# Layer-2 field products in four row strips with a turn of their own on the y banks, and W2 loaded in turned pieces

## The chip, the cores and the metric

One core of a Trainium2 chip runs the whole kernel. The metric is the device time of one execution in microseconds. Engines are named as in the profile: PE is the matrix engine (PEld its weight loads), DVE the vector engine, ACT the scalar engine, POOL the general engine, SP the engine that only issues DMAs.

## What is computed

The input x has 512 rows of 64 fields with 16 elements each. Three layers of a compressed interaction network follow one another; each multiplies the previous layer's channels with all 64 fields, element by element, and mixes the products with a weight matrix of 128 outputs. The output is the sum over the 16 elements of each layer.

```python
for W, b in params:                      # W0: 128 x 64*64, W1 and W2: 128 x 128*64
    z = jnp.einsum('bhd,bfd->bhfd', x_vec, input)
    z = z.reshape(B, h * f, d)
    x_vec = jnp.einsum('oc,bcd->bod', W, z) + b[None, :, None]
    outs.append(x_vec.sum(axis=2))
return jnp.concatenate(outs, axis=1)     # 512 x 384
```

## The kernel before

**Tiling.** A tile is 8 batch rows x 16 elements = 128 columns. Four tiles make a group of 512 columns, and there are 16 groups, each a body that is written out for all engines. In a body the step e runs over 4 tiles x 16 chunks (e = 16 j + c); a chunk is four fields.

**Layer 0** of the next group is spread over the current group: the symmetric products of the fields are made in 17 pieces z (t = 0 to 16). SP copies shifted rows of x into z (L372), POOL multiplies them (L453), ACT and DVE split every second piece into two rounded parts (L526, L718), and PE adds each piece to the PSUM bank l0 at the steps of AHEAD_AT (AHEAD_FIRST_AT in the first group), whole pieces as one f32 matmul (L934), split ones as three rounded ones (L913, tile l).

**Layer 1** is the bulk. For each chunk PE makes y = W1 times x1, three 512-column matmuls (L913, tile y), into one of four PSUM banks. Then the chunk is weighted with its four fields and summed over chunks: chunks in HELPED by ACT into prod (L673) and by POOL into pacc (L461, L463), chunks in SCALED in place by ACT (L662) and added by DVE in one operation (L754), all others by DVE alone, four operations a chunk (L769, L767). PE may write a bank again only when the chunk that was there four chunks ago has been read (chunk, L1042 and L1044). At a tile's end POOL adds acc and pacc and folds them to x2 (combine, L469 to L474).

**Layer 2** needs only sums over elements. For the tile before, at c = 12 (LAYER2_AT), PE multiplies x2 with bd, a copy of the fields masked by batch row, in two halves of 64 partitions, 260 columns each (layer2, L1033), into the two banks of l2p. ACT copies the result into gram and sums (layer2_out, L563 and L565) and makes the next bd in own_rows (L652). Every four groups gram holds 128 batch rows, and PE multiplies it with w2t in 64 f32 matmuls, eight parts of eight (quarter, L1021), which use the bank xt. The turned fields use the same bank (turn_fields, L991, at TURN_AT, directly behind a layer2).

**Weights.** W0, W1 and W2 arrive in rows by output. W0 is folded by DVE (add_pairs, L851) and turned by PE in the front; W1 is turned by PE in 16 chunks in the first tile of the first group (turn_w1, L968), W2 in 16 chunks in the steps 14 to 29 of the first group (turn_w2, L1010, copied out by ACT, L582). SP loads W1 (L387), ACT loads W0 (L512) and, in the first group, W2 (L595).

**The end.** After the last chunk DVE adds pacc (L896) and reduces to x2 (L899); then follow the last layer2, its copy, the last quarter, its copy to sums (L571), three transposes (L1001), their copy (L577) and the store (L419).

## Time and profile before

| what | value |
|---|---|
| time, median of 3 runs | 1092.88 us (1091.29 to 1093.42) |
| the profiled execution's own time | 1091.6 us |
| its span, first to last instruction | 1089.5 us |
| busy share of PE, PEld, DVE, ACT, POOL | 98%, 74%, 81%, 65%, 79% |
| PE share of the chain that ended last | 90% |
| mean granted clock of PE | 0.997 |

The span is the profiled execution from its first to its last instruction; 2.1 us lie around it. Busy time is the union of an engine's instructions. Matmuls are pipelined and the end of one is modelled, so the distance between two starts tells more than one duration. A record of an f32 matmul stands for half of it: one matmul leaves two records.

### The profile page before, as it was taken

Reading aid. Unit: us, or ns where it says so; the run is one execution under the profiler, and the core shown is the slowest. Engines: PE = TensorE matmul, PEld = TensorE weight load, DVE = VectorE, ACT = ScalarE, POOL = GpSimd, SP = SyncE. Lnnn points to the kernel's source line nnn. Section 1 sums busy time; section 2 is a strip of 40 time slices with the busy share of each in tenths; the row PEclk is TensorE's granted clock in tenths of the full one; section 3 lists DMA queues with packets and bytes.
Section 4 is the critical chain, followed back from the end, with each engine's and each line's share of the span. In section 5 each row is a group of like instructions: output and inputs, shape, how many; then the busy total and the mean of one; then the engine's idle time right before and its main releaser. Section 6 shows DMA issues by size and latency. Waiting matters only on the chain.

```text
span 1089.5 us, 18056 instructions
## 1 busy us (share of the span) xinstructions
PE 1064.6 (98%) x4783; PEld 803.5 (74%) x4783; DVE 877.3 (81%) x2673; ACT 710.3 (65%) x2447; POOL 859.6 (79%) x727
## 2 busy tenths in 40 slices
PE   5999999999999999999999999999999999999997
PEld 5777777777778777777778777777778877777676
DVE  5768989889874888989894798989886598888881
ACT  4666767676764767767673676777675576767770
POOL 2668997989884897989985799898987589898550
PEclk9999999999999999999999999999999999999998
DMA  7942423332322323323241232433332133320000
GB/s 275 245 92 81 101 71 71 96 76 78 66 70 58 76 78 69 85 57 97 66 87 40 56 97 66 88 84 69 94 79 59 47 69 97 76 79 28 1 23 8
DMA packets 108327, 85.88 MB, mean 79 GB/s; under 512 B 71040, under 2 KB 73824, under 8 KB 108096
## 3 DMA queue, kind: packets, MB, share of 16 engines
q1 hardware_dynamic: 106832, 78.17, 29.3%
q10 hardware_dynamic: 1392, 6.55, 1.9%
q8 instruction: 38, 0.62, 0.2%
q14 instruction: 65, 0.53, 0.2%
HBM read 14.75 MB, written 0.79 MB: 14 GB/s over the span
## 4 chain that ended last, share of the span: by engine, by line
PE 90%; DVE 3%; ACT 2%; DMA 2%; POOL 1%; issue 1%; ACTq 0%; SPq 0%; DVEq 0%; POOLq 0%
PE y L913 62%; PE l L934 9%; PE l L913 8%; PE xt L1021 5%; PE l2p L1033 4%; DVE acc L769 2%; DMA gram<-in_L_rec_W_dram 1%; PE l2p L1010 1%; ACT y L662 1%; DMA z<-xg 1%; ACT prod L673 1%; POOL z L453 1%; DVE gram L851 1%; PE l L922 0%; POOL pacc L463 0%
## 5 line engine op out<-in xcount | busy, mean ns | idle before, releaser
L769 DVE SCALAR_TENSOR_TENSOR acc<-y,x0t,acc 128x128 f32<-128x128 f32 x2048 | 559.8, 341 | 101.8 <-PE y L913 99.1
L673 ACT ACTIVATE prod<-y,x0t 128x128 f32<-128x128 f32 x1280 | 365.8, 379 | 157.4 <-PE y L913 148.6
L913 PE MATMUL y<-w1h,x1h 128*128 128x512 f32 x1024 | 464.6, 454 | 2.2 <-DVE acc L769 1.4
L913 PE MATMUL y<-w1h,x1l 128*128 128x512 f32 x1024 | 402.1, 393 | 0.0
L913 PE MATMUL y<-w1l,x1h 128*128 128x512 f32 x1024 | 400.6, 391 | 0.0
L453 POOL TENSOR_TENSOR z<-z,xg 128x512 f32<-128x512 f32 (+2 forms) x272 | 352.5, 1300 | 32.8 <-DMA z<-xg 32.8
L463 POOL TENSOR_TENSOR pacc<-pacc,prod 128x512 f32<-128x512 f32 x192 | 268.0, 1396 | 79.7 <-ACT prod L673 78.3
L913 PEld LDWEIGHTS y<-w1h,x1h 128*128 128x128 f32 x1024 | 193.2, 189 | 96.8 <-issue 26.5
L662 ACT ACTIVATE y<-y,x0t 128x128 f32<-128x128 f32 x512 | 142.6, 342 | 157.4 <-PE y L913 157.2
L913 PEld LDWEIGHTS y<-w1l,x1h 128*128 128x128 f32 x1024 | 192.8, 188 | 59.3 <-issue 28.8
L913 PEld LDWEIGHTS y<-w1h,x1l 128*128 128x128 f32 x1024 | 192.1, 188 | 43.0
L754 DVE TENSOR_TENSOR acc<-y,acc 128x512 f32<-128x512 f32 x128 | 88.3, 690 | 64.6 <-ACT y L662 61.4
L718 DVE TENSOR_TENSOR zl<-z,zh 128x512 fp32r<-128x512 f32 (+1 forms) x128 | 126.9, 991 | 7.1 <-ACT zh L526 4.5
L934 PE MATMUL l<-z,w0t 128*128 128x512 f32 (+1 forms) x256 | 128.8, 584 | 0.0
L469 POOL TENSOR_TENSOR pacc<-pacc,acc 128x512 f32<-128x512 f32 x63 | 87.4, 1387 | 42.4 <-DVE acc L754 34.5
L461 POOL TENSOR_TENSOR pacc<-prod 128x512 f32<-128x512 f32 x64 | 90.0, 1406 | 37.7 <-ACT prod L673 37.5
L526 ACT CAST zh<-z 128x512 fp32r<-128x512 f32 (+1 forms) x128 | 81.4, 636 | 10.9 <-POOL z L453 7.7
L652 ACT ACTIVATE bd<-x0t,own_half 128x64 f32<-128x64 f32 x256 | 69.1, 359 | 0.0
L1021 PEld LDWEIGHTS xt<-gram,w2t 128*128 128x128 f32 x512 | 62.3, 195 | 3.6 <-ACT sums L565 1.5
L1021 PE MATMUL xt<-gram,w2t 128*128 128x128 f32 x512 | 62.7, 279 | 0.8 <-ACT sums L565 0.8
L767 DVE TENSOR_SCALAR acc<-y,x0t 128x128 f32<-128x128 f32 x192 | 54.9, 341 | 0.0
L934 PEld LDWEIGHTS l<-z,w0t 128*128 128x128 f32 x256 | 47.8, 188 | 9.6
(85 smaller groups left out, 673.0 us busy)
## 6 DMA issues: line engine op xcount, KB each, us to landing
z<-xg SPq DMA_DIRECT2D x480, 128.0 KB, 2.4
w2t<-in_L_rec_W_dram SPq DMA_DIRECT2D x8, 512.0 KB, 7.1
gram<-in_L_rec_W_dram ACTq DMA_DIRECT2D x8, 512.0 KB, 7.4
xg<-in_r_input_dram SPq DMA_DIRECT2D x30, 128.0 KB, 3.8
z<-xg SPq DMA_DIRECT2D x32, 96.0 KB, 5.9
z<-xg SPq DMA_DIRECT2D x15, 192.0 KB
gram<-in_L_rec_W_dram ACTq DMA_DIRECT2D x1, 2048.0 KB, 9.2
out_dram<-z SPq DMA_DIRECT2D x4, 192.0 KB, 1.9
```

Of the source, the lines that this page charges most:

```text
L453: nc.gpsimd.tensor_tensor(to[0:rows, :], to[0:rows, :], xg[0:rows, cols], ALU.mult).then_inc(z_made, 1)
L461: nc.gpsimd.tensor_tensor(pacc[:], prod[:, 0], prod[:, 1], ALU.add).then_inc(pool_step, 1)
L463: nc.gpsimd.tensor_tensor(pacc[:], pacc[:], prod[:, h % HSLOTS], ALU.add).then_inc(pool_step, 1)
L469: nc.gpsimd.tensor_tensor(pacc[:], pacc[:], acc[:, slot], ALU.add).then_inc(pool_step, 1)
L662: last = nc.scalar.activation(of, of, ACT.Copy, scale=x0t[:, j, f:f + 1])
L673: last = nc.scalar.activation(prod[:, h % HSLOTS, k, :], y[c % YB][:, k * O:(k + 1) * O], ACT.Copy, scale=x0t[:, j, f:f + 1])
L718: nc.vector.tensor_tensor(zl[:, i % ZLSLOTS, cols], zin(n, t), zh[:, zhslot(n, t), cols].bitcast(F32), ALU.subtract).then_inc(zl_made, 1)
L754: nc.vector.tensor_tensor(to, y[c % YB][:], to, ALU.add).then_inc(acc_step, 1)
L769: ins = nc.vector.scalar_tensor_tensor(out=to, in0=of, scalar=x0t[:, j, f:f + 1], in1=b1r[:] if m == 0 else to, op0=ALU.mult, op1=ALU.add)
L913: ins = nc.tensor.matmul(to, stationary, moving, start=(first and k == 0), stop=(last and k == 2))
L934: nc.tensor.matmul(l0[:, cols], w0t[:, WHOLE.index(t), :], zin(n, t), start=(t == 0), stop=False).then_inc(z_used, 1)
L1021: last = nc.tensor.matmul(l2, w2t[:, f, :], gram[:, f, :], start=(f == 0), stop=(f == F - 1))
```

## The change

- The two halves of layer2 become four strips of 32 partitions with 130 columns each. They write to the two banks of l2p, to free columns of the bank that also holds xt (now named spare), and to one y bank. layer2 therefore takes a turn among the four y banks: 17 turns a tile in place of 16 (turn_of, ybank, turn_free). own_rows makes two copies in place of four, layer2_out six copies in place of two. layer2 waits for three more things.
- HELPED is (0, 4, 6, 8, 10) in place of (0, 4, 6, 8, 12), SCALED (3,) in place of (3, 15), in the last group (3, 9, 12) in place of (3, 9). OWN_AT, LOWER_AT, SUM_AT and AHEAD_AT move by one or two steps. TURN_AT moves from step 28 to step 35, where no layer2 stands.
- W2 is no longer turned by PE. From step 68 of the whole run to step 233 ACT loads it in 16 pieces of eight outputs, turned by the DMA's addresses, and copies each into w2t ten steps later. Its staging place is the still unused part of sums.
- First group: layer 0 of group 1 stands at the steps 26 to 55 with its products dealt anew over POOL's steps. ACT issues W1's loads as soon as x has arrived, in place of SP after the first turned fields. DVE's folds of W0 are cut in another way (the parts that are not used are no longer made, 568 sums a step in place of 760; the first step has 56 more). Six transposes whose result is not used follow the first turn of W0.
- End: the last layer2 is copied out by ACT and DVE together; the last quarter has gram and w2t exchanged, so that its rows are those of the output; DVE adds the bias and writes the last third itself; the last reduction is two additions. 24 transposes whose result is not used stand ahead of the last layer2.

```diff
-HALF = P // 2
-HALF_B = TILE_B // 2
+STRIPS = 4
+STRIP = P // STRIPS
+STRIP_B = TILE_B // STRIPS
...
-HELPED = (0, 4, 6, 8, 12)
+HELPED = (0, 4, 6, 8, 10)
 HN = len(HELPED)
 SUMMED = tuple(c for c in range(CHUNKS) if c not in HELPED)
-SCALED = (3, 15)
-SCALED_LAST = (3, 9)
+SCALED = (3,)
+SCALED_LAST = (3, 9, 12)
...
-OWN_AT = 11
-GRAM = HALF_B * F
+OWN_AT = 10
+GRAM = STRIP_B * F
...
+W2_PARTS = 16
 QUARTER_AT = [CHUNKS + 2 + k for k in range(QUARTER_PARTS)]
-LOWER_AT = 4
-SUM_AT = 6
-TURN_AT = LAYER2_AT + CHUNKS
+LOWER_AT = 3
+SUM_AT = 4
+TURN_AT = LAYER2_AT + CHUNKS + 7
 LOWER_AFTER = 2
+LAST_CLOCK_KEEPERS = 24
...
-W2_AT = 14
...
-W2_LOAD_AT = [k * 3 // 2 for k in range(W_PARTS)]
+W2_LOAD_AT = [CHUNKS * TILES + 4 + 11 * k for k in range(W2_PARTS)]
+W2_KEEP_AT = [at + 10 for at in W2_LOAD_AT]
...
-LATER_PRODUCTS = (6, (0, 1, 4, 3, 3))
-AHEAD_AT = [9 + t * 46 // (ZT - 1) for t in range(ZT)]
+LATER_PRODUCTS = (6, (3, 0, 5, 3, 0))
+AHEAD_AT = [7 + t * 47 // (ZT - 1) for t in range(ZT)]
...
-AHEAD_FIRST_AT = [24 + t * 31 // (ZT - 1) for t in range(ZT)]
+AHEAD_FIRST_AT = [26 + t * 29 // (ZT - 1) for t in range(ZT)]
...
-PRODUCTS_FIRST_AT = ((0, 0, 0, 0, 0), (2, 1, 1, 1, 2), (2, 1, 2, 1, 2), (2, 0, 0, 0, 0))
+PRODUCTS_FIRST_AT = ((0, 0, 0, 0, 0), (0, 3, 1, 0, 1), (3, 3, 1, 1, 4), (0, 0, 0, 0, 0))
...
+        spare = ps("spare", [P, CHUNK])
+        xt = spare[:, 0:TILES * F].rearrange("p (t f) -> p t f", f=F)
+        l2 = spare[:, 0:QB]
+        l2p_spare = spare[:, TILES * F:TILES * F + GRAM + STRIP_B]
...
+        def turn_of(j, c):
+            return (CHUNKS + 1) * j + c + (1 if c > LAYER2_AT else 0)
+        def ybank(j, c):
+            return turn_of(j, c) % YB
+        def l2p_bank(j):
+            return l2p_turn(j) % YB
+        def l2p_turn(j):
+            return (CHUNKS + 1) * j + (LAYER2_AT + 1 if j < TILES else 0)
+        def turn_ahead(tile, j, turn):
+            back, at = divmod(turn - YB, CHUNKS + 1)
+            if at == LAYER2_AT + 1:
+                if isinstance(tile, int) and tile - j + back < 1:
+                    return turn_ahead(tile, j, turn - YB)
+                return tile - j + back, None
+            return tile - j + back, at - (1 if at > LAYER2_AT else 0)
...
+            act.wait_ge(x_loaded, 32)
+            for k in range(W_PARTS):
+                part = slice(k * F * O // W_PARTS, (k + 1) * F * O // W_PARTS)
+                act.dma_start(w1raw[:, part], w1[:, part]).then_inc(w1_loaded if k < W1_FIRST else w1_rest_loaded, 16)
...
-                nc.scalar.copy(gram[:, :, bass.ds(to, TILE_B)].rearrange("p f (k b) -> p f k b", k=2),
-                               l2p[:, :, 0:GRAM].rearrange("p k (b f) -> p f k b", f=F))
-                nc.scalar.copy(sums1[:, bass.ds(tile * TILE_B, TILE_B)].rearrange("p (k b) -> p k b", k=2),
-                               l2p[:, :, GRAM:GRAM + HALF_B]).then_inc(l2p_used, 1)
+                own_bank = y[l2p_bank(j)]
+                for at, of, k in ((0, l2p[:], 2), (2, l2p_spare.unsqueeze(1), 1), (3, own_bank[:].unsqueeze(1), 1)):
+                    b = at * STRIP_B
+                    nc.scalar.copy(gram[:, :, bass.ds(to + b, k * STRIP_B)].rearrange("p f (k b) -> p f k b", k=k),
+                                   of[:, :, 0:GRAM].rearrange("p k (b f) -> p f k b", f=F))
+                    last = nc.scalar.copy(
+                        sums1[:, bass.ds(tile * TILE_B + b, k * STRIP_B)].rearrange("p (k b) -> p k b", k=k),
+                        of[:, :, GRAM:GRAM + STRIP_B])
+                last.then_inc(l2p_used, 1)
...
+                part = slice(k * O // W2_PARTS, (k + 1) * O // W2_PARTS)
+                act.dma_start(w2stage, w2[part, :].rearrange("o (h f) -> h o f", f=F)).then_inc(w2_loaded, 16)
+            def keep_w2(k):
+                act.wait_ge(w2_loaded, 16 * (k + 1))
+                part = slice(k * O // W2_PARTS, (k + 1) * O // W2_PARTS)
+                nc.scalar.copy(w2t[:, :, part], w2stage.rearrange("p o f -> p f o")).then_inc(w2_kept, 1)
...
+            act.wait_ge(l2p_made, layer2_ready(GROUPS * TILES - 1))
+            nc.scalar.copy(gram[:, :, QB - TILE_B:QB - 2 * STRIP_B].rearrange("p f (k b) -> p f k b", k=2),
+                           l2p[:, :, 0:GRAM].rearrange("p k (b f) -> p f k b", f=F))
+            nc.scalar.copy(sums1[:, B - TILE_B:B - 2 * STRIP_B].rearrange("p (k b) -> p k b", k=2),
+                           l2p[:, :, GRAM:GRAM + STRIP_B]).then_inc(l2p_used, 1)
+            act.wait_ge(turned, B // P)
+            nc.scalar.copy(outs[:, B // P - 1, 0:(L - 1) * O], l0[:, 0:(L - 1) * O]).then_inc(outs_made, 1)
...
+                near, edge = F - s0, n - 1
+                add_pairs(at(w0pair, F * s0, [F, n], [1, near]),
+                          at(w0stage, s0, [1, n], [F + 1, near]),
+                          at(w0stage, F * s0, [F, n], [F + 1, near]))
+                if r > 0:
+                    add_pairs(at(w0pair, F * s0 + near, [F, n], [1, s0]),
+                              at(w0stage, (F + 1) * near - near, [1, n], [F + 1, s0]),
+                              at(w0stage, (F + 1) * near - F * near, [F, n], [F + 1, s0]))
+                add_pairs(at(w0pair, F + (F - 1) * s0, [F - 1, n], [1, edge]),
+                          at(w0stage, F * F - F * s0, [-F, n], [F + 1, edge]),
+                          at(w0stage, F - s0, [-1, n], [F + 1, edge]))
...
-            nc.vector.tensor_reduce(x2[:, slot], acc[:, slot].rearrange("p k o -> p o k"), AX.X,
-                                    ALU.add).then_inc(x2_made, 1)
+            nc.vector.tensor_tensor(acc[:, slot, 0:2], acc[:, slot, 0:2], acc[:, slot, 2:4], ALU.add).then_inc(acc_step, 1)
+            dve.wait_ge(acc_step, tile_added(tile) + 2)
+            nc.vector.tensor_tensor(x2[:, slot], acc[:, slot, 0], acc[:, slot, 1], ALU.add).then_inc(x2_made, 1)
...
+            own_bank = y[l2p_bank(TILES)]
+            nc.vector.tensor_copy(gram[:, :, QB - 2 * STRIP_B:QB - STRIP_B],
+                                  y[1][:, 0:GRAM].rearrange("p (b f) -> p f b", f=F))
+            nc.vector.tensor_copy(gram[:, :, QB - STRIP_B:QB],
+                                  own_bank[:, 0:GRAM].rearrange("p (b f) -> p f b", f=F)).then_inc(gram_half_made, 1)
...
+            nc.vector.tensor_tensor(outs[:, B // P - 1, (L - 1) * O:L * O], l2, b2r[:], ALU.add).then_inc(last_rows_made, 1)
...
-            def turn_w2(c):
-                if c >= 2:
-                    pe.wait_ge(w2_kept, c - 1)
-                else:
-                    pe.wait_ge(w1l_made, CHUNKS)
-                for k in range(CF):
-                    last = nc.tensor.transpose(l2p[:, c % 2, k * O:(k + 1) * O],
-                                               w2raw.rearrange("o (h f) -> o f h", f=F)[:, CF * c + k, :], ident[:])
-                last.then_inc(w2_turned, 1)
...
+                    if q == 1:
+                        pe.wait_ge(w2_kept, W2_PARTS)
...
+            def turn_free(tile, j, turn):
+                user, c = turn_ahead(tile, j, turn)
+                if c is None:
+                    pe.wait_ge(l2p_used, user + 1)
+                elif c in HELPED:
+                    pe.wait_ge(prod_made, HN * user + HN + HELPED.index(c) + 1)
+                else:
+                    pe.wait_ge(acc_step, added(user, c))
+            def layer2(tile, slot, j, fields_kept, quarters_out):
                 pe.wait_ge(x2_made, x2_ready(tile))
                 pe.wait_ge(bd_made, tile + 1)
                 pe.wait_ge(l2p_used, tile + 1)
-                for k in range(2):
-                    half = slice(k * HALF, (k + 1) * HALF)
-                    last = nc.tensor.matmul(l2p[:, k, 0:GRAM + HALF_B], x2[half, slot], bd[half, slot, :],
+                turn_free(tile + 1, j, l2p_turn(j))
+                pe.wait_ge(x0t_made, fields_kept)
+                pe.wait_ge(l2_used, quarters_out)
+                third = l2p_spare if j < TILES else y[1][:]
+                for k, to in enumerate((l2p[:, 0], l2p[:, 1], third, y[l2p_bank(j)][:])):
+                    rows = slice(k * STRIP, (k + 1) * STRIP)
+                    last = nc.tensor.matmul(to[:, 0:GRAM + STRIP_B], x2[rows, slot], bd[rows, slot, :],
...
-                before, late = (c - YB) % CHUNKS, c < YB
-                if before in HELPED:
-                    value = HN * tile + (HN + HELPED.index(before) + 1) - (HN if late else 0)
-                    pe.wait_ge(prod_made, value)
-                else:
-                    pe.wait_ge(acc_step, added(tile - 1 if late else tile, before))
+                turn_free(tile, j, turn_of(j, c))
...
+            for _ in range(CLOCK_KEEPERS):
+                nc.tensor.transpose(y[W0_STEPS - 2][:, 0:P], ident[:], ident[:])
...
+            pe.wait_ge(outs_made, B // P - 1)
+            for _ in range(LAST_CLOCK_KEEPERS):
+                nc.tensor.transpose(l0[:, (L - 1) * O:L * O], ident[:], ident[:])
+            layer2(GROUPS * TILES - 1, 1, TILES, 2 * GROUPS, QUARTERS)
+            pe.wait_ge(x0t_made, 2 * GROUPS)
+            pe.wait_ge(l2p_used, GROUPS * TILES + 1)
+            pe.wait_ge(gram_half_made, 1)
+            for f in range(F):
+                if f == F // 2:
+                    pe.wait_ge(gram_half_made, 2)
+                    for k in range(L - 1):
+                        last = nc.tensor.transpose(l0[:, k * O:(k + 1) * O], sums[:, k, B - P:B], ident[:])
+                    last.then_inc(turned, 1)
+                last = nc.tensor.matmul(l2, gram[:, f, :], w2t[:, f, :], start=(f == 0), stop=(f == F - 1))
+            last.then_inc(l2_made, 1)
```

## Rows read from the trace of the kernel before

**Rows 1.** Chain that ended last, shares by line

```profile
PE y L913 62%; PE l L934 9%; PE l L913 8%; PE xt L1021 5%; PE l2p L1033 4%; DVE acc L769 2%; DMA gram<-in_L_rec_W_dram 1%; PE l2p L1010 1%; ACT y L662 1%; DMA z<-xg 1%; ACT prod L673 1%; POOL z L453 1%; DVE gram L851 1%; PE l L922 0%; POOL pacc L463 0%
```

**Rows 2.** Windows of 60.5 us in groups 5 and 6, busy time by engine

```profile
382.00:442.50 60.50, 60.50 (x255) 44.73 (x254) 52.95 (x165) 42.50 (x150) 54.16 (x46) 1.00 0.33 78
```

**Rows 3.** Chain in order of time: start, us, what; last runs without layer 0

```profile
117.10 9.44 PE y L913 x39
...
178.92 9.44 PE y L913 x39
...
239.45 9.44 PE y L913 x39
```

**Rows 4.** Timeline of PE around one layer2: start, us, what

```profile
420.06 0.40 PE L913 MATMUL y<-w1h,x1l 128*128 128x512 f32 x1
420.39 0.71 PE L1033 MATMUL l2p<-bd,x 64*128 64x260 f32 x4
...
421.37 0.40 PE L913 MATMUL y<-w1l,x1h 128*128 128x512 f32 x1
421.60 0.39 PE L913 MATMUL y<-w1h,x1l 128*128 128x512 f32 x1
```

**Rows 5.** Timeline of PE, a layer2 with turned fields behind it

```profile
403.34 0.40 PE L913 MATMUL y<-w1h,x1l 128*128 128x512 f32 x1
...
404.88 0.39 PE L913 MATMUL y<-w1l,x1h 128*128 128x512 f32 x1
```

**Rows 6.** Timeline of PE in the first group

```profile
26.17 0.48 PE L913 MATMUL y<-w1h,x1h 128*128 128x512 f32 x1
...
57.24 0.83 PE L1010 MATMUL l2p<-ident,gram 128*128 128x128 f32 x4
...
80.54 0.71 PE L1010 MATMUL l2p<-ident,gram 128*128 128x128 f32 x4
81.18 0.46 PE L991 MATMUL xt<-ident,xg 64*128 64x64 f32 x4
...
81.91 0.40 PE L913 MATMUL y<-w1l,x1h 128*128 128x512 f32 x1
```

**Rows 7.** Timeline of POOL in the first group

```profile
63.54 1.34 POOL L469 TENSOR_TENSOR pacc<-pacc,acc 128x512 f32<-128x512 f32 x1
...
66.20 1.29 POOL L453 TENSOR_TENSOR z<-z,xg 128x512 f32<-128x512 f32 x1
...
121.46 1.31 POOL L469 TENSOR_TENSOR pacc<-pacc,acc 128x512 f32<-128x512 f32 x1
```

**Rows 8.** Groups by form: count, busy us, mean ns, idle before

```profile
L769 DVE SCALAR_TENSOR_TENSOR acc<-y,x0t,acc 128x128 f32<-128x128 f32 x2048 | 559.8, 341 | 101.8 <-PE y L913 99.1
...
L754 DVE TENSOR_TENSOR acc<-y,acc 128x512 f32<-128x512 f32 x128 | 88.3, 690 | 64.6 <-ACT y L662 61.4
...
L563 ACT COPY gram<-l2p 128x512 f32<-128x512 f32 x64 | 38.9, 608 | 6.7 <-PE l2p L1033 6.7
...
L851 DVE TENSOR_TENSOR gram<-gram 128x256 f32<-128x256 f32 x8 | 5.0, 629 | 0.3
```

**Rows 9.** Timeline of the end

```profile
1066.64 1.02 DVE L899 TENSOR_REDUCE x<-acc 128x128 f32<-128x512 f32 x1
...
1067.71 1.24 PE L1033 MATMUL l2p<-bd,x 64*128 64x260 f32 x4 [3.98 <-DVE x L899]
...
1069.71 15.98 PE L1021 MATMUL xt<-gram,w2t 128*128 128x128 f32 x128 [0.75 <-ACT sums L565]
...
1086.75 0.48 ACT L577 COPY z<-l 128x384 f32<-128x384 f32 x1 [0.66 <-PE l L1001]
```

**Rows 10.** Window within the end: PE busy, granted clock

```profile
1066.00:1068.00 2.00, 0.28 (x2) 0.50 0.00 0
```

**Rows 11.** Timeline of PE in the front, transposes alone

```profile
9.92 3.83 PE L945 MATMUL l2p<-ident,z 128*128 128x128 f32 x16 [1.64 <-DVE z L829]
...
15.45 0.66 PE L955 MATMUL y<-ident,gram 128*128 128x128 f32 x4 [0.61 <-DVE gram L851]
```

127 lines of the change are left out of this document (59 added, 68 removed).

## The prediction

> **What bounds the kernel now.** I read the chain that ended last first: PE's y matmuls hold 62% of it, all of PE 90% [rows 1]. Then the windows of a steady group: in 60.5 us PE is busy for all 60.5, DVE for 53.0, ACT for 42.5 and POOL for 54.2 [rows 2]. The same stretch returns after 61.82 us in group 1 and after 60.53 us in group 2 [rows 3]. So in the steady groups a gain has to shorten PE's own list, and DVE and POOL come next, with 7.5 and 6.3 us of air a group. The first group is another stage: its first chunk starts at 26.17 [rows 6] and its chunk 61 at 117.10 [rows 3], 90.9 us, where a steady group has 60.5 less three chunks, 58.5 us. These 32 us are W1's and W2's turns, its own layer 0, and waits.
>
> **Layer2 in four strips.** The last y matmul ahead of a layer2 starts at 420.06 and the second one behind it at 421.37; less two slots of 0.23 (421.37 to 421.60), layer2 costs PE 0.85 us [rows 4]. An f32 matmul costs about four times a rounded one of the same size (a whole piece of layer 0 has 9% of the chain over 128 pieces, 0.77 us [rows 1], a rounded one 0.23), so two with 260 columns one after the other would need 2 x 4 x 260 columns at 2.4 GHz, 0.87 us, and their weights on top. Their four records lie within 0.71 us, with the drain of the last: the two halves of the partitions run side by side. So about 0.43 us of the 0.85 is columns, and 0.42 is the step into the half-height mode and back, with weights loaded in the open. Four strips side by side have 130 columns: 0.22 us, 0.22 less. Bounds: if only two run at a time, nothing is gained; if none do, 0.43 us are lost each. I take the gain, as two already overlap. 60 layer2 of groups 1 to 15: -13.0 us; three in the first group are counted below.
>
> The three added waits sit in PE's sequencer. All three are for things done well before (the bank read four turns ago, fields copied some steps before, a quarter long out), so I take 0, bound 0.1 us each time.
>
> **Turned fields at step 35.** Now they share the mode change with a layer2: 403.34 to 404.88 is 1.54 us, less two slots 1.09, less layer2 0.24 for themselves [rows 5]. Alone they cost more: in the first group, behind four weight turns that start at 80.54 and end near 81.07, the second y starts at 81.91; less one slot 0.61 to 0.63 [rows 6]. So moving them costs 0.38 us in each of 14 groups: +5.4 us. This part works against the strips.
>
> **DVE, ACT and the banks.** A tile now has one chunk more for DVE alone and one scaled chunk less. Four operations take 4 x 559.8 / 2048 = 1.09 us, the single one 0.69 [rows 8]: +0.40 us a tile, 1.6 a group, DVE 54.6 of 60. ACT loses a scaled chunk and two of bd, gains four small copies: less work. But chunks 11 to 15 are now five in a row on DVE, and where no layer 0 lies between (steps 55 to 63 and 0 to 6) PE makes a chunk in 0.68 us. Laid out by hand with these durations, DVE's release of a bank is 0.1 to 0.3 us late for chunks 2 and 3 of the next group; the kernel before also loses some 0.5 us a group there (39 matmuls in 9.44 us [rows 3], where 39 x 0.23 are 8.9). I take +0.25 us a group more, 15 groups, +3.8 us (bounds 0 and +8).
>
> The layer2 result stands in a y bank until ACT has made six copies. A copy of 512 elements takes 0.61 us [rows 8]; six small ones are between 1.2 and 1.6 us. PE wants that bank again after three chunks, 2.04 us. Hidden, with about 0.5 us to spare where layer 0 is absent.
>
> W2's 16 pieces cost ACT a DMA issue and a copy of 512 elements each, in groups 1 to 3. ACT has 18 us free a group [rows 2], but in pieces of 1 to 2 us. +1.5 us (0 to +5). The transfers have ten steps, 9 us, to land.
>
> **First group and front.** The turns of W2: from the first at 57.24 to the fifteenth at 80.54 [rows 6] are 23.3 us with 14 turns. The other work is 14 chunks of 0.68, two whole pieces and one split piece of layer 0; by the chain's 9% and 8% over 128 pieces each 0.77 and 0.68 [rows 1]: 11.7 us. So a turn costs 0.83 us, sixteen 13.2. Three layer2: -0.65. Front: DVE's folds take 0.63 us for 256 sums [rows 8] and a quarter fewer are made, about -1.1; W1 is asked for earlier, for which no row here gives a price: I take 1.1 more (bounds 0 and 2), -2.2 together. With W2's 4 MB out of the way of layer 0's copies, I take 2 us of the waits in the W1 part. Sum -18.
>
> What is late next is POOL. Between the combine of tile 0 (63.54) and that of tile 3 (121.46) it now has 57.9 us [rows 7]. After the change it has three combines of 2.6, twelve additions of 1.3 and 17 products of 1.29 there, 45 us, and 12 of the products fall into tile 2, where PE needs only 18 us for its own list and POOL 24. ACT's casts wait for these products ahead of the multiplications that free y banks. I give back 3 us: -15 (bounds -9, if POOL keeps its hold on both tiles, and -19, if nothing is given back).
>
> **The end.** Reduction of 1.02 us in two additions, -0.35. The last layer2 takes 1.24 us [rows 9] at a granted clock of 0.50, that is 1.2 GHz [rows 10]; at 2.4 GHz and in strips about 0.6, -0.6. Copies shared, -0.15. The quarter takes 15.98 us, its start at the low clock; 64 f32 matmuls of 128 columns are 64 x 4 x 128 columns at 2.4 GHz, 13.7 us, with some 0.01 us between them 14.3, plus two transposes: -1.5. From the quarter's end, 1085.69, to the end of L577, 1087.23, lie 1.5 us [rows 9], replaced by one addition of 0.3: -1.2. Sum -3.8 (bounds -2 and -5). The 24 transposes run while DVE finishes (PE now stands idle for 4 us there) and cost nothing as long as they end before x2, some 2.6 us of work.
>
> These last two terms need the clock to stay up on transposes alone. In the front there is nothing but transposes: 17 starts in 3.83 us, 0.21 us apart, and later four within 0.66 us, 0.11 apart [rows 11]. So PE went from 1.2 to 2.4 GHz after transposes only, and I take the clock as held. The Trainium skill says otherwise: in "TensorE: Matmul & The Clock Gate", Part 4, transposes do not count as PE work in the same way and do not bring the full clock. By that rule 1.7 us of the end's gain would be missing; the trace's front disagrees.
>
> **Sum.** 1091.6 (the profiled execution, 1.3 below the median of 1092.88) -15 -13.0 +5.4 +3.8 +1.5 -3.8 = 1070.5 us. All lower bounds together give 1060, all upper ones 1086.
>
> **Rivals.**
> - Keepers without effect (0.10): the clock falls in PE's pause as it does now [rows 10], and 1.7 us of the end are missing, 1072. Against: [rows 11].
> - POOL holds the first group (0.15): PE waits at ACT's casts in tiles 1 and 2, the first part brings 7 us: 1078.5. For it: POOL's 24 us of work in tile 2. Against: 12 us of air in [rows 7].
> - Strips run two at a time (0.08): the 13 us are missing, 1083.5. Against: nothing in [rows 4] says that two is the limit.
> - The bank turn (0.08), the other side: 17 turns on four banks. ACT comes to the six copies late (a cast waiting for a product, or W2), and chunk 0 of the next tile waits, in every tile. From 0.35 us a tile over 60 tiles it eats the whole gain; at 0.5 us it is +30, 1100. For it: five DVE chunks in a row, POOL at 90% [rows 2]. Against: three chunks of PE work cover 2 us.
> - The forecast 0.57 (own range 1064 to 1077); changes nothing 0.02.
>
> The measurement tells 0.2%, 2.2 us, from no change. Faster 0.90 (all but the bank turn, and some of the mishaps together), same 0.02, slower 0.08. The range 1061 to 1085 holds the forecast, the two-strip and the POOL cases.
>
> **What would show it.** Right: four strips starting together with 0.1 us to the second set; groups 60.2 us apart; chunk 61 of the first group near 100; no L1010; granted clock 1.00 to the end. Wrong: waits of PE for ACT's gram copies at chunk 0, POOL without a gap up to 120 us, or groups longer than 60.5 us, which would mean that DVE or the banks have become the bound.

## The result, and the profile after

The change makes the kernel faster by about half of what was forecast: a median of 1082.57 us (1079.72 to 1085.28) beside 1092.62 for the kernel before, ratio 0.9909 with a 95% interval of 0.9881 to 0.9937. The forecast was 1070.5 us, ratio 0.979. Run again (e1 below), the changed kernel gave 0.9896 (0.9883 to 0.991).

The page of the profiled execution (time 1079.72, span 1078.0) has as its first lines the busy time by engine, and as its fourth part the chain that ended last:

```profile
PE 1054.0 (98%) x5004; PEld 796.2 (74%) x5004; DVE 911.5 (85%) x2848; ACT 649.0 (60%) x2346; POOL 866.9 (80%) x727
...
PE 71%; DVE 9%; ACT 2%; issue 2%; POOL 0%; DVEq 0%; ACTq 0%; POOLq 0%
PE y L982 48%; PE l L1003 8%; DVE acc L817 8%; PE l L982 7%; PE spare L1082 4%; PE spare L1196 2%; PE l2p L1108 1%; ACT y L706 1%; ACT prod L717 1%; DVE x1l L783 1%; PE spare L1060 0%; POOL pacc L494 0%; DVE acc L802 0%; PE l L991 0%; ACT bd L696 0%
```

DVE's additions (now L817) have gone from 2% of the chain [rows 1] to 8%. PE is still busy for 98% of the span, but it no longer sets the time alone. Now stage by stage. The first y of each chunk in PE's timeline marks a chunk's start; the table gives what passes from the first chunk of a group to that of the next (group 15: to its last chunk), each in one profiled execution. Groups 4, 8 and 12 hold a quarter.

```
us          before   after  after, again
first start  26.17   25.13   25.58
group 0      93.05   83.58   82.48
group 1      61.83   61.02   61.04
groups 2, 3  60.53 60.48   60.81 61.05   60.82 61.05
group 4      74.85   74.61   74.60
groups 5-7   60.57 60.51 60.51   61.01 60.25 60.26   61.00 60.25 61.02
group 8      74.85   74.60   75.37
groups 9-11  60.57 60.47 60.53   60.23 60.25 61.03   61.03 61.00 60.26
group 12     74.83   74.59   75.39
groups 13-14 60.51 60.53   60.27 60.25   60.25 60.26
group 15     52.00   54.20   54.27
then to end  26.74   24.81   23.20
```

The groups have two lengths after the change, 60.25 and 61.0 (with a quarter 74.6 and 75.4), and which group is the long one differs from one execution to the next. The last group is longer than before by 2.2 us.

**Layer2.** The timeline of PE around one layer2, which answers to [rows 4]:

```profile
424.24 0.39 PE L982 MATMUL y<-w1h,x1l 128*128 128x512 f32 x1
424.56 0.38 PE L1108 MATMUL l2p<-bd,x 32*128 32x130 f32 x2
424.57 0.37 PE L1108 MATMUL spare<-bd,x 32*128 32x130 f32 x1
424.58 0.37 PE L1108 MATMUL y<-bd,x 32*128 32x130 f32 x1
424.78 0.28 PE L1108 MATMUL l2p<-bd,x 32*128 32x130 f32 x2
...
425.33 0.39 PE L982 MATMUL y<-w1l,x1h 128*128 128x512 f32 x1
```

Each f32 matmul leaves two records, so the four strips show as two sets of four. The first set starts within 0.02 us, the second 0.22 later. From 424.24 to 425.33, less two slots, is 0.63 us where 0.85 stood before. The turned fields alone, answering to [rows 5], take 401.00 to 402.05 less two slots, 0.59 us, as had been read from [rows 6] (0.61 to 0.63):

```profile
401.00 0.39 PE L982 MATMUL y<-w1h,x1l 128*128 128x512 f32 x1
401.32 0.46 PE L1060 MATMUL spare<-ident,xg 64*128 64x64 f32 x4
401.71 0.50 PE L982 MATMUL y<-w1h,x1h 128*128 128x512 f32 x1
402.05 0.39 PE L982 MATMUL y<-w1l,x1h 128*128 128x512 f32 x1
```

**Front.** PE's last matmul ahead of the turns of W1 (L985 before, L1054 after) starts at 22.07 before and at 20.95 after. Then PE stands still until the first of these turns. The view of the line that issues W1's loads, before and after, and the first turn:

```profile
L387 SPq DMA_DIRECT2D w2t<-in_L_rec_W_dram x8: 327/505/1606, 8.6 to 13.6; - x8
DMA to landing us min/median/max: 3.8/7.1/9.6
23.26 1.42 PE L968 MATMUL l2p<-ident,w2t 128*128 128x128 f32 x8 [0.89 <-issue]
```

```profile
L549 ACTq DMA_DIRECT2D w2t<-in_L_rec_W_dram x8: 359/480/547, 4.3 to 7.9; - x8
DMA to landing us min/median/max: 8.2/10.9/14.3
22.23 1.42 PE L1037 MATMUL l2p<-ident,w2t 128*128 128x128 f32 x8 [0.98 <-issue]
```

The last piece is issued at 13.57 and takes 9.6 us before the change (23.17), and is issued at 7.86 and takes 14.3 us after it (22.14). Both times the first turn follows 0.09 us behind this landing, and so it does in the profiles of all runs. (W1 lies in the place of w2t, so the rows have that name.)

**First group.** L1010's turns are gone. PE now stops twice before its chunk 16, and then runs at 1.2 GHz for a while (timeline of PE; then windows of 2 us with busy times of PE, PEld, DVE, ACT, POOL and the granted clock):

```profile
54.21 0.50 PE L982 MATMUL y<-w1h,x1h 128*128 128x512 f32 x1 [0.61 <-DVE w1l L825]
...
56.85 0.77 PE L982 MATMUL y<-w1h,x1h 128*128 128x512 f32 x1 [1.67 <-issue]
```

```profile
54.00:56.00 2.00, 0.96 (x3) 0.48 (x3) 2.00 (x9) 0.00 (x0) 0.00 (x0) 1.00 0.81 192
56.00:58.00 2.00, 1.15 (x3) 0.99 (x4) 2.00 (x6) 0.00 (x0) 0.00 (x0) 0.56 0.82 200
58.00:60.00 2.00, 2.00 (x7) 1.57 (x6) 0.53 (x3) 1.14 (x4) 1.46 (x2) 0.58 0.81 208
```

From 54 to 58 DVE is busy without a break: PE waits for W1's last lower part (L825), then for the lower part of x1 (L783, done at 56.75), which stand behind DVE's additions. The second of these waits was there before, with 0.46 us (59.78, ahead of the same chunk, 0.10 us behind the end of x1's lower part both times). Later, from 71 to 97 us, the waits of all engines are led by ACT's casts, which wait for POOL's products:

```profile
ACT zh L563 <- POOL z L486: 11.6, 4, 4.2
DVE zl L766 <- ACT zh L563: 3.5, 3, 2.1
```

**Last group.** In three of its four tiles PE stands for 0.6 us ahead of layer2 and waits for DVE's addition of a scaled chunk:

```profile
1049.93 0.39 PE L982 MATMUL y<-w1h,x1l 128*128 128x512 f32 x1
1050.92 0.38 PE L1108 MATMUL l2p<-bd,x 32*128 32x130 f32 x2 [0.60 <-DVE acc L802]
```

**End.** It answers to [rows 9] and [rows 10]:

```profile
1053.95 2.78 PE L1185 MATMUL l<-ident 128*128 128x128 f32 x24
1058.02 0.38 PE L1108 MATMUL l2p<-bd,x 32*128 32x130 f32 x2 [1.29 <-DVE x L956]
...
1059.23 9.01 PE L1196 MATMUL spare<-w2t,gram 128*128 128x128 f32 x64 [0.70 <-DVE sums L966]
1068.08 0.38 PE L1194 MATMUL l<-ident,sums 128*128 128x128 f32 x2
1068.30 7.31 PE L1196 MATMUL spare<-w2t,gram 128*128 128x128 f32 x64
```

The first 64 matmuls take 9.01 us and the second 64 take 7.31: in this execution the clock fell to 0.50 in the window from 1060 to 1062. In the second run's profile it stayed at 1.00, both halves took 7.38 and 7.31, and the stretch from the last chunk to the end was 23.20 us instead of 24.81.

So against the forecast (in the profiled executions, which differ by 11.6 us of span): front -1.0 (forecast -2.2), chunks 0 to 14 of the first group -2.7 (-2), the rest of it -6.7 (-10.8), groups 1 to 14 -1.3 (-1.9; in the second run +1.8), group 15 +2.2 (-0.6), the end -1.9 with the fall of the clock and -3.5 without (-3.8).

### The profile page after: what moved, and what is told of

Its sections match the earlier page's. It is cut to its first block, busy times and chain, and to the rows that moved or that the text cites. A ratio compares the mean times of both kernels' runs of the same rounds, so it can differ in the third digit from the quotient of the medians.

```text
span 1078.0 us, 18723 instructions
## 1 busy us (share of the span) xinstructions
PE 1054.0 (98%) x5004; PEld 796.2 (74%) x5004; DVE 911.5 (85%) x2848; ACT 649.0 (60%) x2346; POOL 866.9 (80%) x727
## 4 chain that ended last, share of the span: by engine, by line
PE 71%; DVE 9%; ACT 2%; issue 2%; POOL 0%; DVEq 0%; ACTq 0%; POOLq 0%
PE y L982 48%; PE l L1003 8%; DVE acc L817 8%; PE l L982 7%; PE spare L1082 4%; PE spare L1196 2%; PE l2p L1108 1%; ACT y L706 1%; ACT prod L717 1%; DVE x1l L783 1%; PE spare L1060 0%; POOL pacc L494 0%; DVE acc L802 0%; PE l L991 0%; ACT bd L696 0%
## 5 line engine op out<-in xcount | busy, mean ns | idle before, releaser
L817 DVE SCALAR_TENSOR_TENSOR acc<-y,x0t,acc 128x128 f32<-128x128 f32 x2272 | 620.7, 341 | 92.8 <-PE y L982 86.1
L486 POOL TENSOR_TENSOR z<-z,xg 128x512 f32<-128x512 f32 (+2 forms) x272 | 362.1, 1336 | 21.6 <-DMA z<-xg 21.5
L496 POOL TENSOR_TENSOR pacc<-pacc,prod 128x512 f32<-128x512 f32 x192 | 263.9, 1375 | 45.1 <-ACT prod L717 40.6
L766 DVE TENSOR_TENSOR zl<-z,zh 128x512 fp32r<-128x512 f32 (+1 forms) x128 | 135.2, 1056 | 5.5 <-ACT zh L563 4.9
L706 ACT ACTIVATE y<-y,x0t 128x128 f32<-128x128 f32 x288 | 80.5, 347 | 73.6 <-PE y L982 73.5
L494 POOL TENSOR_TENSOR pacc<-prod 128x512 f32<-128x512 f32 x64 | 87.5, 1367 | 37.8 <-ACT prod L717 37.7
L802 DVE TENSOR_TENSOR acc<-y,acc 128x512 f32<-128x512 f32 x72 | 49.6, 689 | 26.8 <-ACT y L706 25.9
L504 POOL TENSOR_TENSOR pacc<-pacc 128x256 f32<-128x256 f32 x63 | 51.3, 814 | 4.9
L982 PE MATMUL l<-zh,w0h 128*128 128x512 f32 (+1 forms) x128 | 50.8, 397 | 0.0
L982 PE MATMUL l<-zl,w0h 128*128 128x512 f32 (+1 forms) x128 | 49.7, 388 | 0.0
```

Source lines behind the costliest of these rows:

```text
L486: nc.gpsimd.tensor_tensor(to[0:rows, :], to[0:rows, :], xg[0:rows, cols], ALU.mult).then_inc(z_made, 1)
L494: nc.gpsimd.tensor_tensor(pacc[:], prod[:, 0], prod[:, 1], ALU.add).then_inc(pool_step, 1)
L496: nc.gpsimd.tensor_tensor(pacc[:], pacc[:], prod[:, h % HSLOTS], ALU.add).then_inc(pool_step, 1)
L706: last = nc.scalar.activation(of, of, ACT.Copy, scale=x0t[:, j, f:f + 1])
L766: nc.vector.tensor_tensor(zl[:, i % ZLSLOTS, cols], zin(n, t), zh[:, zhslot(n, t), cols].bitcast(F32), ALU.subtract).then_inc(zl_made, 1)
L817: ins = nc.vector.scalar_tensor_tensor(out=to, in0=of, scalar=x0t[:, j, f:f + 1], in1=b1r[:] if m == 0 else to, op0=ALU.mult, op1=ALU.add)
```

## The experiments

Runs e1 to e4 shared one chip, e5 to e8 another, e9 to e11 a third, e12 a fourth; each ratio is to the kernel before, run beside them. Runs e1 to e4 are the changed kernel and edits of it. A step is the time from the first y of one chunk to that of the next; what is said of steps and groups is read from one profiled execution of each kernel.

**e1, the changed kernel again.**

> The changed kernel unchanged, again, as the base for the others of this call and to see how far its executions spread. Theory A (a race between DVE and POOL): each inner group runs at 60.25 us or at 61.0, by whether DVE's subtraction for the split piece of step 11 (0.69 us alone, 1.3 to 1.8 beside a POOL operation) gets ahead of POOL's addition; then the time differs from execution to execution by several times 0.75 us, 1079 to 1086, and the profile has a number of groups near 61.0 other than the 6 of the first one. Theory B (the chip or the run order): the kernel before spreads as much.

Measured: 1081.54 us (1080.6 to 1083.85), ratio 0.9896 (0.9883 to 0.991). Its groups are in the table. Besides group 1, eight are long, against four in the first profile. So theory A's groups are there. The spread of executions is a weaker sign: 3.3 us here and 5.6 in the first run, but the kernel before, with nine executions beside this one, has 2.1.

What makes a group long is seen where two groups of one execution part ways: at the layer2 of step 14. The timeline there, group 5 (long) and then group 6 (short) of the changed kernel:

```profile
377.06 0.63 ACT L563 CAST zh<-z 128x512 fp32r<-128x512 f32 x1
...
377.79 1.83 DVE L766 TENSOR_TENSOR zl<-z,zh 128x512 fp32r<-128x512 f32 x1
377.81 1.26 POOL L496 TENSOR_TENSOR pacc<-pacc,prod 128x512 f32<-128x512 f32 x1
...
438.79 0.69 DVE L766 TENSOR_TENSOR zl<-z,zh 128x512 fp32r<-128x512 f32 x1
438.82 1.81 POOL L496 TENSOR_TENSOR pacc<-pacc,prod 128x512 f32<-128x512 f32 x1
```

DVE's zl and a POOL addition start 0.02 to 0.03 us apart, and one of the two is held up by the other: zl takes 1.83 us and POOL 1.26, or zl 0.69 and POOL 1.81. In this profile zl wins where its recorded start is 0.03 us or more ahead of POOL's and loses at 0.02 or less; in e1, e2 and e4 both happen at 0.02 to 0.03. When zl loses, the bank of chunk 12 comes free late, and PE's chunks 14 and 15 take 0.62 and 0.11 us more.

**e2, turned fields back at step 28, ahead of layer2** (behind it was not tried: there PE would write the spare bank while ACT still copies layer2's result out of it).

```diff
-TURN_AT = LAYER2_AT + CHUNKS + 7
+TURN_AT = LAYER2_AT + CHUNKS
...
-                        pe.wait_ge(l2p_used, n * TILES + 2)
+                        pe.wait_ge(l2p_used, n * TILES + 1)
...
+                    if e == TURN_AT and kind != "last":
+                        turn_fields()
...
-                        if e == TURN_AT:
-                            turn_fields()
```

> The turned fields go back to step 28, directly ahead of layer2 in place of behind it, so that they share its change into the half-height mode. Theory A (the mode change is what they pay at step 35, 0.63 us alone against 0.24 in company): every group of 1 to 14 becomes 0.35 to 0.4 us shorter, 5 us in all. Rival (DVE and the banks set the pace by now): PE gets there earlier and waits for a bank, under 2 us.

Measured: 1081.96 us, ratio 0.9898 (0.9883 to 0.9912), the same as e1. The short groups are 60.08 us instead of 60.25, so the fields cost 0.17 us less in company, not the 0.38 of the prediction; the long ones are 60.84 and group 1 is 62.39. In the groups with a quarter it is the other way: the short one is 75.01 instead of 74.6, for step 27 is 0.5 us longer, where PE waits for ACT's copy of the quarter's result, and so is step 28:

```profile
848.80 0.47 PE L982 MATMUL y<-w1h,x1h 128*128 128x512 f32 x1 [0.34 <-ACT sums L613]
```

So neither theory A's 5 us nor its 0.35 a group came.

**e3, zl one step later.**

```diff
-PARTED_AT = [{AHEAD_AT[t] - k: t for t in PARTED} for k in (5, 4)]
+PARTED_AT = [{AHEAD_AT[t] - k: t for t in PARTED} for k in (5, 3)]
```

> DVE's subtractions for the split pieces one step later in the groups 1 to 14, so that in tile 0 it comes behind chunk 12 and not ahead of it. Theory A (the slow groups lose 0.73 us because chunk 12 is read late behind a subtraction that POOL holds up): no group near 61.0 for steps 14 and 15, time 1 to 5 us less and the spread of executions smaller, under 3 us. Rival (it only moves the wait): the piece of layer 0 comes late and PE waits there, groups as long or longer.

Measured: 1078.37 us (1077.82 to 1078.51), ratio 0.9863 (0.985 to 0.9877). From group 5 on every group is 60.5 (with a quarter 74.6), and the executions lie within 0.7 us instead of 3.3. Step 14 is quick in all groups; step 33 is 0.27 us slower in all of them, which is the price of the later zl there. So the hold-up between zl and POOL is the cause of the long groups. The rival's wait for the piece of layer 0 is there too, but at one place and smaller.

**e4, chunk 5 instead of chunk 9 scaled by ACT in the last group.**

```diff
-SCALED_LAST = (3, 9, 12)
+SCALED_LAST = (3, 5, 12)
```

> In the last group chunk 5 is scaled by ACT in place of chunk 9. Theory A (layer2 now takes a turn on the y banks and waits there for chunk 9, which ACT scales first and DVE adds then, 0.5 us in each of four tiles): the last group becomes 1.5 to 2 us shorter. Rival (the last group is bound by DVE's sum of work): the step at layer2 gets shorter and others longer, under 0.5 us.

Measured: 1080.12 us (1077.48 to 1083.61), ratio 0.9881 (0.9862 to 0.9899). Group 15 falls from 54.27 to 52.44 us. The steps with layer2 at chunks 28, 44 and 60 fall from 1.96 to 1.21 us each; chunks 24, 40 and 56, whose banks are now the late ones, take 1.5 us more together, and chunks 8 and 12 together 0.7 less. The gain is read from the group; the medians of e1 and e4 lie within each other's spread.

Then e3's move for one step only, as the base of all that follows:

**e5, one zl moved.**

```diff
-PARTED_AT = [{AHEAD_AT[t] - k: t for t in PARTED} for k in (5, 4)]
+PARTED_AT = [{AHEAD_AT[t] - (k - 1 if t == 3 and k == 4 else k): t for t in PARTED} for k in (5, 4)]
```

> Of the subtractions that the run before this one moved by a step, only the one of step 11 (t = 3) goes to step 12; it is the base for the other runs of this call. Theory A (one overtaking at this place makes the slow groups): every inner group at 60.25 us, none at 61.0, and no stall of 0.28 us at step 33, so 3 us less than with all moved: about 1075.5, executions within 1.5 us. Rival (the overtaking happens at other split pieces as well): groups still differ among themselves by 0.5 us or more.

Measured: 1074.91 us (1073.79 to 1077.37), ratio 0.9841 (0.9827 to 0.9854). Groups 5 to 14 are all 60.25 or, with a quarter, 74.6, as theory A has it, and the time is near its 1075.5. But the executions lie 3.6 us apart, not within 1.5. The timeline at the same place in group 5: zl starts 0.25 us ahead of POOL's next operation and wins.

```profile
376.50 0.84 DVE L766 TENSOR_TENSOR zl<-z,zh 128x512 fp32r<-128x512 f32 x1
376.75 1.74 POOL L486 TENSOR_TENSOR z<-z,xg 128x512 f32<-128x512 f32 x1
```

**e6, no keepers:** the loop of 24 transposes ahead of the last layer2 (L1184 and L1185) is taken out of e5.

> The base of this call without the 24 transposes ahead of the last layer2; their result is not used. Theory A (transposes keep the clock up): the clock falls to 0.5 in PE's pause of some 4 us, as in the kernel before, the quarter takes 16 us in place of 14.7, layer2 is slower too, and all executions are 1.5 to 2 us longer than the base. Rival (by the rule that transposes do not count, the clock is not theirs to keep): no difference beyond 0.5 us.

Measured: 1076.54 us, ratio 0.9853 (0.984 to 0.9867). The windows of its end:

```profile
1054.00:1056.00 2.00, 1.25 (x11) 1.11 (x12) 0.71 (x5) 0.44 (x2) 0.00 (x0) 0.77 0.00 0
1056.00:1058.00 2.00, 2.00 (x12) 2.00 (x11) 0.00 (x0) 0.00 (x0) 0.00 (x0) 0.50 0.00 0
1058.00:1060.00 2.00, 2.00 (x18) 2.00 (x18) 0.00 (x0) 0.00 (x0) 0.00 (x0) 0.88 0.00 0
```

After a pause of 3.96 us the clock falls, PE works at 1.2 GHz for a while, and the end takes 24.76 us where e5 has 23.20, as theory A has it. The medians lie 1.6 us apart, but the executions overlap (1075.67 to 1077.71), so the profiles carry this reading.

**e7, lower part of x1 first:** in the first group `lower(0, LAST)` is called ahead of the sums of step 14 instead of behind them, on e5.

> In the first group DVE makes x1l for the tiles 1 to 3 ahead of its additions of chunk 14 and not behind them. Theory A (at step 16 PE waits for x1l, which lies behind DVE's backlog from W1, and this wait eats the first four removed turns of W2): step 16 starts 1 us earlier, no fall of the clock there, group 0 shorter by 1 to 2.5 us, if POOL does not take it back in tile 2. Rival (POOL's hold in tile 2 sets the end of group 0 whatever is won ahead of it): step 16 earlier, group 0 the same within 0.3 us.

Measured: 1074.89 us, ratio 0.9841 (0.9828 to 0.9855), nothing won. The step of chunk 15 is 1.03 us shorter (1.61 for 2.64), the steps of chunks 18, 19 and 27 are 0.45, 0.12 and 0.47 longer: the wait is passed on. Its profile also has 1.1 us from a fall of the clock at 24.8 us for 3.4 us, ahead of all this. Chunks 53 and 54 are 0.5 us shorter for another reason: in e5 a zl at 97.0 us lost against POOL (1.78 us), here the same one won (0.68).

**e8, the products of the first group dealt out anew,** on e5: more of them ahead of the combine of tile 0, fewer in tile 2's last step.

```diff
-PRODUCTS_FIRST_AT = ((0, 0, 0, 0, 0), (0, 3, 1, 0, 1), (3, 3, 1, 1, 4), (0, 0, 0, 0, 0))
+PRODUCTS_FIRST_AT = ((0, 0, 0, 0, 0), (2, 2, 1, 1, 1), (3, 3, 1, 1, 2), (0, 0, 0, 0, 0))
```

> In the first group POOL makes products of group 1 ahead of the combine of tile 0, while it now waits 8 to 9 us for DVE there: (2, 2, 1, 1, 1) and (3, 3, 1, 1, 2) in place of (0, 3, 1, 0, 1) and (3, 3, 1, 1, 4). Theory A (POOL's work in tile 2 holds ACT's casts and PE, 3.4 us): group 0 shorter by 2 to 3 us, the steps 34 to 49 without most of their waits. Rival (DVE's backlog at steps 14 to 18 and the banks set group 0): under 0.5 us.

Measured: 1075.09 us (1073.17 to 1075.38), ratio 0.9836 (0.9822 to 0.9849). The medians don't tell it from e5; in the profiles the first group is 81.39 us for 82.82, between the theory and the rival, and 0.7 of this lies at chunks 53 to 55, where e7 won 0.5 without this edit.

**e9, three edits together** (those of e4, e7 and e8, on e5).

> The version of one moved DVE step (1074.9 us) with three edits at once: the lower part of the first group's x1 split ahead of the sums of step 14, the first group's chunks dealt out as in the run of early products, and chunk 5 instead of 9 with ACT's scaled products in the last tile of each quarter's turn. Theory (each wait is a price of its own): -1.5 in the first group from the products, -1.8 in the last group from the bank turn, 0 from the lower part: 1071.6 us, last group 52.4 us, first group 81.4 us. Rival (POOL holds the first group, so what the early products win is lost in its tile 2): first group 82.9 us, 1073.1 us. Second rival (chunk 5 costs in the inner groups what it wins in the last): inner quiet groups above 60.3 us, 1074 us or more.

Measured: 1072.23 us (1071.29 to 1072.85), ratio 0.9813 (0.98 to 0.9827); first group 81.33, last 52.44. It is the fastest version that computes the reference, by the ratios 9 to 10 us faster than the changed kernel, and near its forecast of 1071.6. The second rival could not come true: the edit sets the scaled chunks of the last group alone.

**e10, W2 left out.** In e5 the loads and copies of W2's 16 pieces (`load_w2`, `keep_w2`) and the wait for them are removed; the quarters' products are then not the reference's.

> Leaves out part of the computation: the sixteen loads and copies of W2 in groups 1 to 3, so the quarters' products read what is not W2; all else is the version of one moved DVE step (1074.9 us). My forecast had 1.5 us for ACT's share of W2. Theory now: ACT is late only where a copy falls right ahead of layer2's sums, in group 1 at step 60 (+0.8): group 1 falls from 61.0 to 60.25 us, groups 2 and 3 stay, 1074.1 us. Rival of the forecast: groups 1 to 3 each lose about 0.5, 1073.4 us. Rival nothing: group 1 is long because it follows the first group's lost lead, and stays at 61.0.

Measured: 1074.29 us (1074.0 to 1075.43), ratio 0.9835 (0.9821 to 0.9848). Beside e5 the median is within the spread, but group 1 falls from 61.03 to 60.29, groups 2 and 3 together stay (120.48 for 120.34). So ACT's share of W2 costs 0.7 us, at the one place where a copy stands right ahead of layer2's copies.

**e11, eight wide matmuls as keepers,** on e5.

```diff
-LAST_CLOCK_KEEPERS = 24
+LAST_CLOCK_KEEPERS = 8
...
-                nc.tensor.transpose(l0[:, (L - 1) * O:L * O], ident[:], ident[:])
+                nc.tensor.matmul(l0[:], x1h[:, 0:P], w1h[:, 0, :], start=True, stop=True)
```

> The 24 transposes ahead of the last layer2 become 8 matmuls of 128x512 (3.1 us of TensorE instead of 2.8), on the version of one moved DVE step (1074.9 us). Theory: the transposes are work for the clock already; the end stays at 23.2 us after the last chunk's start when no dip falls there, 1074.9 within 0.8. Rival (only wide matmuls hold the clock; the transposes win only by luck): the transposes' end has a dip of 3.4 us worth 1.6 in some executions and the wide ones' never, so the median falls by about 0.8 to 1074.1 and the spread of executions shrinks.

Measured: 1076.48 us (1075.57 to 1077.04), ratio 0.9852 (0.9839 to 0.9866): no better than no keepers, and neither the theory nor the rival. The timeline of PE and a window (the window of the timeline starts at 1052, so its first row counts five of the eight):

```profile
1051.63 1.31 PE L1185 MATMUL l<-w1h,x1h 128*128 128x512 f32 x5
1055.01 0.38 PE L1108 MATMUL l2p<-bd,x 32*128 32x130 f32 x2 [2.07 <-DVE x L956]
```

```profile
1058.00:1060.00 2.00, 2.00 (x14) 2.00 (x13) 0.00 (x0) 0.00 (x0) 0.00 (x0) 0.62 0.00 0
```

They ended sooner than I had reckoned (the expectation's 3.1 us took the record of one, 0.39 us, for its slot, 0.23), so PE stood for 2.07 us instead of 1.29 ahead of layer2, and the clock fell. Such matmuls are what PE does all through the run with the clock up, so I put the fall down to the longer pause, not to their kind; no run compares the two kinds at equal length.

**e12, POOL freed in the first group.** On e9, POOL's sums and the first two steps of its combines in tiles 0 to 2 go over 8 columns, and x2 there is made of DVE's sums alone, so the result of these tiles is not the reference's.

> Leaves out part of the computation: in the first three tiles GpSimd's sums of ACT's products and the first two steps of the combine go over 8 columns instead of 512 and 256, and x2 is the sum of two chunks' sums of DVE alone; on the version of the three edits together (1072.2 us, first group 81.33 us). In that version GpSimd works without a pause from 55.7 to 97.4 us, and its sums and combines hold 25 us of that. Theory (GpSimd holds tiles 1 and 2 of the first group by 3.4 us, which is what the earlier start of the first group gives back): first group 77.9 us, 1068.8 us. Rival (the first group's later steps are bound by DVE and by TensorE's own work; GpSimd's wait is on paper): first group 81.3 us, 1072.2 us within 0.5. Between them, DVE's part takes over from GpSimd: 79.5 us.

Measured: 1069.15 us (1068.03 to 1070.46), ratio 0.9787 (0.9774 to 0.9801), 3.1 us below e9 by the medians and 2.8 by the ratios, between the theory and DVE's part. The first group is 78.84 us for 81.33, although its clock fell in its first steps, which cost 0.7; the steps of chunks 27 to 49 have become 2.9 us shorter. The edit also takes away most of what POOL reads while DVE works there; that share was not parted off. In e9 POOL works without a pause from 55.67 to 98.2 us; here it waits again for transfers:

```profile
67.48 1.28 POOL L486 TENSOR_TENSOR z<-z,xg 128x512 f32<-128x512 f32 x1 [1.94 <-DMA z<-xg]
```

## Why the direction was right and the size was not

**Strips: right.** 0.22 us less for a layer2 was forecast and measured. The rival that only two strips run at a time is out: they start within 0.02 us. The sign named for it was a second set 0.1 us later, and it came 0.22 later; what lies between the two no row shows.

**Turned fields alone: mis-sized.** Alone they take 0.59 us, as read from [rows 6]. But e2 shows that moving them cost 0.17 us in a group without a quarter, not 0.38, and won 0.4 in one with a quarter: for eleven and three groups some 0.7 us in all where 5.4 were charged. What they add beside a layer2 of four strips is some 0.4 us, more than the 0.24 beside one of two halves.

**DVE and the banks: right in kind, wrong in what was left out.** A short group takes 60.25 us, against 60.53. Four times -0.22 and +0.17 leave +0.43 for the banks, where 0.25 was forecast; this is a remainder and no run shows it by itself. The step that failed is that the durations of DVE's operations were taken as fixed: "Laid out by hand with these durations". zl has no fixed duration. With 128x512 its 120 operations take from 0.68 to 1.83 us in the first profile, and in the changed order it stands ahead of the addition that frees chunk 12's bank, within 0.03 us of a POOL operation. The trace of before had this in it, in the view of zl's line L718 (ns, shortest, median, longest):

```profile
L718 DVE TENSOR_TENSOR zl<-z,zh x128: 546/756/1823, 30.5 to 999.2; 128x512 fp32r<-128x512 f32 x120, 128x384 fp32r<-128x384 f32 x8
```

There, too, zl often started within 0.03 us of a POOL operation, and lost once (1.82 us at 736.6), but the groups were 60.47 to 60.57: a lost race cost nothing there. The long groups cost some 0.77 us each, four to eight of them in the two profiles. From e1 to e5 the profiled spans differ by 6.3 us, the groups 1 to 14 by 6.0 of it. In the second profile this is the largest part of the miss, in the first one, with 3 us, the second after the first group. It is part of the spread of the executions: 0.7 us in e3, but still 3.6 in e5, whose profile has no long group behind group 1; there the two executions with a mean clock of 1.000 are the fastest. The Trainium skill has the rule, in "SBUF — State Buffer", section "Who interferes with whom": a DVE instruction with two inputs in SBUF contends with a GpSimd instruction that reads SBUF, the shared port is an exclusive lock, and the order of issue decides who blocks. The rows agree on the contention and its size, 1.83 beside 1.26 us, or 0.69 beside 1.81. On the order they say less: zl's recorded start is the earlier one in both cases.

**Last group: a wait was priced at nothing.** "The bank read four turns ago ... I take 0, bound 0.1 us each time." In the last group chunk 9 goes by way of ACT and DVE's L802, and layer2's bank is the one of chunk 9. It waits 0.6 us in three tiles, and e4 shows 0.75 for each and 1.8 us for the group. This is the bank turn of the fourth rival, at layer2 itself instead of the chunk behind it, and in one group only. The large wait at chunk 8 is not new: its step has 2.20 us and had 0.69 before, but the step of chunk 10 had 2.27 and has 0.68. It waits for DVE's additions behind the sums of layer 0, and moved with them (SUM_AT). Some 1 us of the 2.8 that the group missed by stays open.

**First group: half right.** The turns of W2 are gone, and POOL was named as late next. Between chunk 14 and the end of the group 62.7 us were to become 51.9, and the profile shows 55.97. Three things were wrong, and their shares overlap.
- The price of a turn, 0.83 us, was not all turn. In the kernel before a chunk with a turn and no wait takes 1.25 us (the two y rows below), one without a turn 0.68, so a turn is 0.57; the rest of the 13.2 us, some 4 us, are waits. Those for ACT's copies of the turned pieces go with the turns. The one for DVE ahead of chunk 16 does not: it was 0.46 and is 1.67. (A whole piece of layer 0, taken as 0.77, costs 0.89 in the steps; that moves the sum by 0.2.)

```profile
64.29 0.48 PE L913 MATMUL y<-w1h,x1h 128*128 128x512 f32 x1
65.54 0.47 PE L913 MATMUL y<-w1h,x1h 128*128 128x512 f32 x1
66.96 0.85 PE L1010 MATMUL l2p<-ident,gram 128*128 128x128 f32 x4 [0.47 <-ACT w2t L582]
```

- DVE was not named. It has W1's lower parts, the additions and x1's lower part at chunks 14 to 16, and PE waits there for 0.61 and 1.67 us. e7 shows that the order of DVE's work isn't the cure, the wait passes to later steps.
- POOL's hold was priced at 3 us. From e5 to e8 the stretch is 1.4 us shorter (some 0.5 of it perhaps zl's race near 97 us, as in e7), from e9 to e12 3.2, to 51.33 us: about 4 in all. The forecast without the 3 us was 48.9, so even with POOL freed some 2 us are missing.

In the first profile the clock falls behind DVE's waits, and chunks 16 and 17 take 1.2 us more than in e5, where it stays up. But this is not part of the miss: chunks 27, 28, 53 and 54 take 1.7 us less than in e5, and the whole stretch is 55.98 in e5. The 0.8 us by which e5's first group is shorter (82.82 for 83.58) lie ahead of chunk 14, and nothing here shows their cause.

**Front: two gains in a row that lie side by side.** Forecast were -1.1 for the folds and -1.1 for W1 asked for earlier; measured is -1.03 together. The folds' operations on DVE fell from 7.8 to 6.6 us, and PE was done with layer 0 1.1 us earlier. But PE then waits for W1's last piece, before and after, and that lands 1.03 us earlier although it is issued 5.7 us earlier. So the landing of W1 sets the start of the first chunk: the term for W1 came (1.03 of 1.1), and the folds' gain disappears in the pause. In e10 and e11, where the last matmul ahead of the turns starts at 22.0 and 22.6, the turn still follows 0.09 us behind the landing. "For which no row here gives a price" was true of the size; the view of L387 would have named the landing.

**W2 on ACT.** 1.5 us forecast, 0.7 measured (e10).

**End, and the clock.** -3.8 forecast, -3.5 measured where the clock stays up. It does not always do so: in the first profile it fell in spite of the transposes, in the ten other profiles of kernels with them it did not. Of e5's four executions two have a mean clock of 1.000; without the transposes none of four has, and the median is 1.6 us higher. So transposes do count as work for the clock, and the prediction's reading of [rows 11] holds; that they always keep it up does not. The Trainium skill, in "TensorE: Matmul & The Clock Gate", Part 4, says that they do not count the same way; e5 and e6 disagree, 23.20 us against 24.76.

**The sum.** In the first profile the terms missed by about 9.8 us: the front 1.2, the W1 part -0.7, the rest of the first group 4.1, groups 1 to 14 0.6, group 15 2.8, the end 1.9. The 0.6 is made of four long groups, 3.1, less 4.7 that the fields and 0.8 that W2 were charged too much, and of a remainder of some 3 us, which falls to the banks and is not shown. In the second run eight groups are long, 3 us more; the clock stays up at the end, 1.6 us less, and the first group is 1.1 us shorter. So the direction and the strips came by the mechanism forecast, and the small miss of the groups 1 to 14 in the first profile is luck: larger errors cancel in it. Of the signs named ahead, the groups were 60.25 to 61.0 apart and not 60.2, chunk 61 of the first group came at 106.5 and not near 100, the clock did not stay at 1.00, and groups longer than 60.5 were named as the sign that DVE or the banks have become the bound.

What is not settled: why a short group needs 0.43 us for the banks where 0.25 was reckoned, the last 2 us of the first group, and some 1 us of the last one.

## What to carry to other kernels

When a schedule is laid out by hand, the duration of a vector operation with two SBUF inputs beside a busy GpSimd is a range, not a number (here 0.68 to 1.83 us for the 128x512 form of L766): keep it away from the start of GpSimd's work, or give it a clear head start, and look at the shortest, median and longest duration in the trace of before. Two gains on one path add up only if nothing else ends last beside them: look for the landing of a transfer as well. A price taken from a stretch has the waits of that stretch in it; ask of each wait whether it goes with the work that is removed. Before a wait is priced at nothing, follow it in each kind of group, the last one too, back to who frees the bank. And moving one step of one engine's list brought 6 us by the ratios (e1 to e5), where the whole change had brought 10 to 12: measure the stage lengths first, then mend what makes one longer than its like.
